# Second block's probabilities split before they are turned, and turned by DMA; score maxima turned by one matmul; places moved

## The chip, the cores and the metric

The kernel runs on one NeuronCore of a Trainium2 chip. The metric is the time of one execution on the device in microseconds (us), lower is better; the time of a kernel is the median of several runs. The engines are TensorE (PE), VectorE (DVE), ScalarE (ACT), GpSimd (POOL) and SyncE (SP), which here only issues DMAs. They run side by side and meet at semaphores.

## What is computed

Eight samples of 512 tokens by 512 channels pass through two transformer blocks. Block 0 has 16 heads of 32 channels and weights rounded to three values; block 1 has one head of 512 channels and full-precision weights. Cut to what matters here:

```python
# block 0: per head, scores by softmax, then values
attn = softmax(einsum('bhqd,bhkd->bhqk', q, k) * hd ** -0.5)
o = einsum('bhqk,bhkd->bhqd', attn, v)
# block 1: one head
Q = h @ q_w + q_b;  K = h @ k_w + k_b;  V = h @ v_w + v_b
attn = softmax(einsum('bnd,bmd->bnm', Q, K) * D ** -0.5)
x = x_in + (einsum('bnm,bmd->bnd', attn, V) @ proj_w + proj_b)
x = x + gelu(film(rmsnorm(x)) @ mlp_w1 + mlp_b1) @ mlp_w2 + mlp_b2
```

## The kernel before, in words

The samples are pipelined: `both(i, j)` on every engine issues block 0 of sample i mixed with block 1 of sample j = i − 1. So there is one pass with block 0 alone, seven mixed ones, and one with block 1 alone. The order of each engine's work is written out by hand: tables such as `S_AT`, `PT_AT`, `PROJ_AT` or `M_AT` give a place (c, n) to each job of block 1, and each engine walks the same list of slots, 24 for c = 0 and 16 for each of c = 1 to 4. In a slot TensorE issues one product of scores by query (L1193; four heads a chunk c, four blocks of 128 queries each), from c = 1 on also one by key (L1243), at set slots the products of probabilities and values (L1278), and what the tables put there. VectorE takes the maximum of each row of scores by query: of two products at once (L1202) for the first 24, of one (L1205) after. ScalarE takes the exponential of each product by key (L1250). The remainder of each probability beyond bf16 is formed on POOL or on VectorE (L1261), as `EXTRA_DVE`, `EXTRA_POOL` and `FIRST_DVE` say: 24 of 64 on VectorE.

The maxima must lie along the free dimension before the scores by key are made. `turn_maxima` turns them with four fp32 transposes of 128×4 (L1212), `max_high` (ACT, L1219) and `max_low` (DVE, L1226) split the turned 4×512 into two bf16 parts, and `stack_maxima` (SP, L1232 and L1234) copies each part by DMA into one row of the stacked queries.

Block 1 works in split bf16: each product is three matmuls a quarter (high by high, high by low, low by high: L1430 to L1432), so an output of 128×512 takes twelve. Its softmax has four row blocks t. `s1` makes the scores, `max1` (L1572 to L1579, DVE) the maximum, `exp_1` (L1589, ACT) the exponential into `wide[t % 2]` in fp32 with its sum. `turn_p1` turns it by four fp32 transposes of 128×128 on TensorE into a PSUM bank (L1600), `p_high` (L1605, ACT) copies that as bf16 and `p_low` (L1611, DVE) subtracts, and `proj1` multiplies both parts with the values. The jobs of block 1 take turns on banks 6 and 7. `exp_1` of t ≥ 2 waits until block t − 2 was turned out of `wide`.

SP issues its DMAs in one order: the weight units of 1 MB (`load_unit`, L1418), for each chunk the parts of queries and keys out to DRAM (L1144, L1146) and back in stacked form (L1155, six), the maxima, and in the MLP of block 0 the transposing DMA of `turn_hidden` (L1380, 128×2048 bf16, 512 KB), which is the only transpose by DMA in the kernel before. POOL forms the values' low parts (`value_low`, L1184) ahead of the remainders.

The wait by which `exp_1` frees its buffer, and the transposes:

```python
            if t >= 2:
                ready(act, plan1, ("pT", t - 2), i)
...
            for k in range(TT):
                mm = pe.transpose(banks[:, b, k * P:(k + 1) * P], wide[:, t % 2, k * P:(k + 1) * P], ident)
```

## Time and profile before

| | us |
|---|---|
| median of 3 runs | 2208.48 |
| lowest, highest | 2206.46, 2213.61 |
| the profiled execution, its own time | 2211.1 |
| its span in the profile | 2209.3 |

The mean granted clock of TensorE in the profiled execution is 0.973 of full speed. The profile gives each engine's busy time, a table of stretches, the chain of work that ended last, groups of instructions by line, and every instruction in order of time. Starts are microseconds from the span's first instruction; "idle before" is what the engine stood idle ahead of an instruction, with the instruction that released it. Instructions overlap: the start of the next one, not the duration, says what one costs its engine.

### The profile page before, as it was taken

How to read it: one execution, taken by the hardware profiler on the slowest of the kernel's cores; microseconds unless marked ns; L12 is line 12 of the kernel's file. 1: busy time of each engine (PE TensorE's matmuls, PEld its weight loads, DVE VectorE, ACT ScalarE, POOL GpSimd, SP SyncE). 2: the span in 40 equal slices, each digit the busy share in tenths (PEclk: the TensorE clock that was granted, in tenths of full speed). 3: DMA queues.
4: the chain of work that ended last, by engine and by line, in shares of the span. 5: the costliest groups of instructions: out<-in, count | busy, mean ns of one | idle time of the engine just before them, and what ended most of it. 6: DMA issues, size and time to landing. Idle time of an engine off the chain costs nothing.

```text
span 2209.3 us, 34388 instructions
## 1 busy us (share of the span) xinstructions
PE 1975.2 (89%) x12991; PEld 981.8 (44%) x12991; DVE 1537.1 (70%) x2667; ACT 1088.2 (49%) x1962; POOL 807.1 (37%) x705
## 2 busy tenths in 40 slices
PE   4787868899988998899988998899988998899989
PEld 3354334544444444544444444544444444544434
DVE  5666567885788767875788767875788767875422
ACT  4475543753456443753456343753456343753230
POOL 2173433741246213741245213741246213741021
PEclk8899889999999999999999999999999999999999
DMA  8442552023321333023321333023321332013212
GB/s 307 146 164 105 191 195 100 26 87 96 129 73 40 105 115 101 26 88 96 132 68 40 107 113 101 26 87 96 131 71 40 109 111 101 26 62 97 91 38 96
DMA packets 152027, 216.97 MB, mean 98 GB/s; under 512 B 74172, under 2 KB 115424, under 8 KB 139704
## 3 DMA queue, kind: packets, MB, share of 16 engines
q1 hardware_dynamic: 144088, 191.66, 26.3%
q10 hardware_dynamic: 7776, 23.10, 2.8%
q8 instruction: 106, 1.74, 0.3%
q14 instruction: 57, 0.47, 0.1%
HBM read 161.97 MB, written 35.72 MB: 89 GB/s over the span
## 4 chain that ended last, share of the span: by engine, by line
PE 55%; DVE 25%; ACT 9%; issue 6%; POOL 3%; DMA 1%; SPq 0%; ACTq 0%; DVEq 0%; POOLq 0%
PE banks L1430 10%; PE banks L1432 10%; PE banks L1431 10%; PE banks L1388 5%; PE banks L1331 4%; DVE memory L1205 4%; PE banks L1278 4%; DVE memory L1202 3%; PE banks L1243 2%; DVE memory L1016 2%; ACT memory L1250 2%; PE banks L1102 2%; PE banks L1193 2%; PE banks L1313 1%; DVE memory L1031 1%
## 5 line engine op out<-in xcount | busy, mean ns | idle before, releaser
L1430 PE MATMUL banks<-memory 128*128 128x512 bf16 x1536 | 586.1, 382 | 25.9 <-DVE memory L1678 5.9
L1431 PE MATMUL banks<-memory 128*128 128x512 bf16 x1536 | 585.5, 381 | 0.0
L1432 PE MATMUL banks<-memory 128*128 128x512 bf16 x1536 | 585.1, 381 | 0.0
L1261 POOL TENSOR_TENSOR memory<-memory 128x512 bf16<-128x512 f32 x332 | 375.4, 1151 | 371.0 <-ACT memory L1250 370.0
L1250 ACT ACTIVATE memory<-banks 128x512 f32<-128x512 f32 x512 | 290.4, 598 | 131.3 <-PE banks L1243 129.1
L1656 POOL TENSOR_TENSOR memory<-memory 128x512 bf16<-128x512 f32 x128 | 153.8, 1204 | 459.1 <-DVE memory L1651 459.1
L1193 PE MATMUL banks<-memory 96*128 96x512 bf16 x512 | 188.6, 395 | 72.8 <-DVE memory L1205 41.4
L1430 PEld LDWEIGHTS banks<-memory 128*128 128x128 bf16 x1536 | 150.7, 98 | 215.3 <-issue 40.0
L1205 DVE TENSOR_REDUCE memory<-banks 128x1 f32<-128x512 f32 x320 | 207.6, 679 | 42.4 <-PE banks L1193 41.9
L1432 PEld LDWEIGHTS banks<-memory 128*128 128x128 bf16 x1536 | 150.8, 98 | 184.0 <-issue 4.4
L1431 PEld LDWEIGHTS banks<-memory 128*128 128x128 bf16 x1536 | 150.9, 98 | 170.5 <-issue 3.5
L1243 PE MATMUL banks<-memory 98*128 98x512 bf16 x512 | 187.6, 391 | 13.3 <-ACT memory L1250 6.7
L1645 ACT ACTIVATE memory<-banks,memory 128x512 f32<-128x512 f32 x128 | 87.5, 684 | 205.1 <-PE banks L1432 135.2
L1678 DVE TENSOR_TENSOR memory<-banks,memory 128x512 f32<-128x512 f32 x128 | 88.2, 689 | 121.3 <-PE banks L1432 120.8
L1278 PEld LDWEIGHTS banks<-memory 128*128 128x128 bf16 x4096 | 145.7, 100 | 47.0 <-issue 24.2
L1261 DVE TENSOR_TENSOR memory<-memory 128x512 bf16<-128x512 f32 x180 | 141.4, 818 | 35.8 <-ACT memory L1250 35.1
L1278 PE MATMUL banks<-memory 128*128 128x66 bf16 x4096 | 152.0, 197 | 14.8 <-issue 12.4
L1651 DVE CAST memory<-memory 128x512 bf16<-128x512 f32 x128 | 67.8, 542 | 93.1 <-ACT memory L1645 92.1
L1331 PE MATMUL banks<-memory 128*128 128x512 fp8e4 x512 | 118.8, 386 | 13.6 <-issue 10.2
L1202 DVE TENSOR_REDUCE memory<-banks 128x2 f32<-128x1024 f32 x96 | 116.8, 1217 | 17.9 <-PE banks L1193 17.1
L1388 PE MATMUL banks<-memory 128*128 128x512 fp8e4 x512 | 118.0, 384 | 8.4 <-DMA memory<-memory 8.4
L1470 POOL TENSOR_TENSOR memory<-memory 128x512 f32<-128x512 f32 x64 | 80.5, 1272 | 119.2 <-DVE memory L1078 112.1
(173 smaller groups left out, 2775.4 us busy)
## 6 DMA issues: line engine op xcount, KB each, us to landing
memory<-weight_parts SPq DMA_DIRECT2D x80, 1024.0 KB, 4.8
memory<-head_parts SPq DMA_DIRECT2D x192, 128.0 KB, 2.6
head_parts<-memory SPq DMA_DIRECT2D x64, 256.0 KB, 2.2
memory<-in_x SPq DMA_DIRECT2D x32, 256.0 KB, 3.4
memory<-ada_rows SPq DMA_DIRECT2D x16, 512.0 KB, 4.5
memory<-in_L_cond_w_fc ACTq DMA_DIRECT2D x2, 4096.0 KB, 14.9
memory<-in_L_cond_mlp_w SPq DMA_DIRECT2D x8, 1024.0 KB, 9.2
weight_parts<-memory SPq DMA_DIRECT2D x8, 1024.0 KB, 5.8
```

The source lines that it names most:

```text
L1193: mm = pe.matmul(banks[:, b], q_stack[0:STACK, c % STACKS, j, t * P:(t + 1) * P], k_stack[0:STACK, c % STACKS, j], start=True, stop=True)
L1202: dve.tensor_reduce(neg_max[:, c % 2, t - 1:t + 1, j], banks[:, b - 1:b + 1], AX.X, ALU.max, negate=True).then_inc(free[b].sem, 1)
L1205: dve.tensor_reduce(neg_max[:, c % 2, t, j:j + 1], banks[:, b], AX.X, ALU.max, negate=True).then_inc(free[b].sem, 1)
L1243: pe.matmul(banks[:, b], k_stack[0:rows, c % STACKS, j, kt * P:(kt + 1) * P], q_stack[0:rows, c % STACKS, j], start=True, stop=True).then_ ...
L1250: act.activation(expo[:, e % RING], banks[:, b], ACT.Exp, scale=HEAD_SCALE).then_inc(free[b].sem, 1)
L1261: eng.tensor_tensor(prob_lo[:, e % RING], expo[:, e % RING], prob_hi[:, e % RING], ALU.subtract).then_inc(ok.sem, 1)
L1278: mm = pe.matmul(banks[:, b, at:at + VALUE], part[:, (h * TT + kt) % RING, t * P:(t + 1) * P], values[:, kt, h], start=(kt == 0 and part i ...
L1331: mm = pe.matmul(banks[:, b], xq[:, k, t * P:(t + 1) * P], w0_fc1[:, k, n * D:(n + 1) * D], start=(k == 0), stop=(k == KC - 1))
L1388: mm = pe.matmul(banks[:, b], hid_turned[t % 2][:, f], w0_fc2[:, f], start=(f == 0), stop=(f == FC - 1))
L1430: pe.matmul(bank, lh, rh, start=(k == 0), stop=False)
L1431: pe.matmul(bank, lh, rl, start=False, stop=False)
L1432: mm = pe.matmul(bank, ll, rh, start=False, stop=(k == KC - 1))
```

## The change

The second block's exponentials are no longer turned in fp32. `p_high` (now on DVE) copies the upper 16 bits of each of `wide`'s words as the high part, `p_low` (now on POOL) subtracts that from the word as the low part, both into a free part of `big`, 128×1024 bf16 for each row block; `turn_p` on SP turns both parts by one transposing DMA of 256 KB into `act_k`, where `proj1` reads them. `exp_1` waits for both parts instead of the turned bank, and the plan has no "pT" jobs. `turn_maxima` turns the 128×16 maxima by one transpose; the parts are split as 16×128. On SP the four transposing DMAs stand behind the third weight unit of a pass, between spill and stack of chunk 2, and ahead of the first maxima. Scores and output products of block 1 can be given in quarters; all quarters of one stand at one slot. Many places move by some slots, and VectorE forms 20 of the 64 remainders.

```diff
-LATE_QK = {(0, 6): ("q", 2), (0, 12): ("k", 2), (1, 3): ("q", 3), (1, 6): ("k", 3)}
+LATE_QK = {(0, 4): ('q', 2), (0, 12): ('k', 2), (1, 2): ('q', 3), (1, 8): ('k', 3)}
...
-M_AT = ((3, 8), (3, 11), (3, 14), (4, 1), (4, 4), (4, 7), (4, 10), (4, 13))
+M_AT = ((3, 11), (3, 13), (3, 15), (4, 2), (4, 3), (4, 5), (4, 9), (4, 15))
...
-TURN_AT = ((2, 7), (2, 9), (2, 11), (2, 13))
-NORM_AT = ((1, 14), (1, 15), (2, 0), (2, 1))
-SQUARE_AT = ((1, 4), (1, 6), (1, 8), (1, 10))
-PT_AT, PT_READ = (((0, 3), (0, 10), (0, 15)), ((0, 2), (0, 11), (0, 14)))
-S_AT = ((0, 4), (0, 7))
-PROJ_AT, PROJ_READ = (((0, 16), (0, 21), (1, 0), (1, 5)), ((0, 15), (0, 22), (0, 23), (1, 5)))
+TURN_AT, FILM_FULL, FILM_HIGH, FILM_LOW = (((2, 5), (2, 7), (2, 9), (2, 12)), ((2, 5), (2, 7), (2, 9), (2, 12)), ((2, 6), (2, 8), (2, 10), (2, 13)), ((2, 7), (2, 9), (2, 11), (2, 14)))
+NORM_AT = ((1, 14), (1, 15), (2, 0), (2, 2))
+SQUARE_AT = ((1, 0), (1, 1), (1, 5), (1, 11))
+PARTS_AT = ((0, 2), (0, 11), (0, 15))
+S_AT, S_MAX, S_EXP = (((0, 4), (0, 4), (0, 4), (0, 4), (0, 8), (0, 8), (0, 8), (0, 8)), ((0, 4), (0, 8)), ((0, 4), (0, 8)))
+PROJ_AT, PROJ_READ = (((0, 16), (0, 16), (0, 16), (0, 16), (0, 20), (0, 20), (0, 20), (0, 20), (1, 0), (1, 0), (1, 0), (1, 0), (1, 5), (1, 5), (1, 5), (1, 5)), ((0, 17), (0, 20), (0, 23), (1, 5)))
...
-MAX_AT = {(0, 17): 0, (1, 8): 1, (2, 11): 2, (3, 10): 3}
+MAX_AT = {(0, 18): 0, (1, 9): 1, (2, 9): 2, (3, 9): 3}
...
-EXTRA_DVE = (17, 22, 25, 30, 34, 38)
-EXTRA_POOL = (48, 52, 56, 60)
+EXTRA_DVE = (12, 14, 17, 23, 34, 38, 39)
+EXTRA_POOL = (46, 48, 49, 50, 54, 56, 57, 60, 62)
...
             b = take(pe, plan0, ("max", c), i)
-            for t in range(TT):
-                mm = pe.transpose(banks[0:G, b, t * P:(t + 1) * P], neg_max[:, c % 2, t], ident)
-            mm.then_inc(full[b].sem, 1)
+            pe.transpose(banks[0:HEADS, b, 0:P], neg_max[:, c % 2].rearrange("p j t -> p (j t)"), ident
+                         ).then_inc(full[b].sem, 1)
...
-            act.activation(max_hi[0:G], banks[0:G, b], ACT.Copy).then_inc(max_parts.sem, 1)
+            act.activation(max_hi[0:HEADS, 0:P], banks[0:HEADS, b, 0:P], ACT.Copy).then_inc(max_parts.sem, 1)
...
             if t >= 2:
-                ready(act, plan1, ("pT", t - 2), i)
+                act.wait_ge(p_hi_ok.sem, p_hi_ok(i, t - 1))
+                act.wait_ge(p_lo_ok.sem, p_lo_ok(i, t - 1))
...
-        def turn_p1(pe, i, t):
-            done(pe, plan1, ("s", t), i)
-            b = take(pe, plan1, ("pT", t), i)
-            for k in range(TT):
-                mm = pe.transpose(banks[:, b, k * P:(k + 1) * P], wide[:, t % 2, k * P:(k + 1) * P], ident)
-            mm.then_inc(full[b].sem, 1)
...
+        def p_high(dve, i, t):
+            done(dve, plan1, ("s", t), i)
+            dve.tensor_copy(p_parts[:, t, 0], wide_hi[:, t % 2]).then_inc(p_hi_ok.sem, 1)
+
+        def p_low(pool, i, t):
+            done(pool, plan1, ("s", t), i)
+            pool.tensor_tensor(p_parts[:, t, 1], wide[:, t % 2], wide_hi[:, t % 2], ALU.subtract
+                               ).then_inc(p_lo_ok.sem, 1)
+
+        def turn_p(sp, i, t):
+
+            sp.wait_ge(p_hi_ok.sem, p_hi_ok(i, t + 1))
+            sp.wait_ge(p_lo_ok.sem, p_lo_ok(i, t + 1))
+            out = act_k[:, :, :, t * P:(t + 1) * P].rearrange("p s k n -> p (s k) n")
+            sp.dma_start_transpose(out, p_parts[:, t].rearrange("p s n -> p (s n)")).then_inc(p_in[t].sem, 16)
...
+                pe.wait_ge(p_in[t].sem, p_in[t](i, 16))
...
                 units(j, 3, 4)
+                if j is not None:
+                    for t in range(2):
+                        turn_p(sp, j, t)
                 if i is not None:
                     spill_parts(sp, i, 2)
+                if j is not None:
+                    turn_p(sp, j, 2)
+                if i is not None:
                     stack_parts(sp, i, 2)
+                if j is not None:
+                    turn_p(sp, j, 3)
+                if i is not None:
                     stack_maxima(sp, i, 0)
...
+                    if j is not None:
+                        p_low(pool, j, 0)
                     for t in range(TT):
                         value_low(pool, i, t)
+                if j is not None:
+                    for t in range(0 if i is None else 1, TT):
+                        p_low(pool, j, t)
...
-                lows1(j, [("s", 1), ("pT", 0)])
+                lows1(j, [("p", 0), ("s", 1)])
...
-                products1(j, [("s", 1), ("pT", 0)])
+                products1(j, [("s", 1)])
```

## Rows read from the trace of the kernel before

**Rows 1.** The page, part 1: busy time, share of the span, instructions

```profile
PE 1975.2 (89%) x12991; PEld 981.8 (44%) x12991; DVE 1537.1 (70%) x2667; ACT 1088.2 (49%) x1962; POOL 807.1 (37%) x705
```

**Rows 2.** Stretches of one sample: from:to, length, busy us (instructions), PEclk, DMA

```profile
1097.00:1127.00 30.00, 24.32 (x117) 10.98 (x115) 25.04 (x36) 6.86 (x15) 2.63 (x3) 1.00 0.38 124
1127.00:1192.00 65.00, 56.27 (x663) 32.41 (x663) 54.85 (x108) 51.46 (x106) 45.95 (x42) 0.95 0.07 22
1192.00:1310.00 118.00, 115.72 (x588) 54.03 (x585) 80.49 (x131) 50.35 (x85) 32.44 (x30) 1.00 0.32 101
```

**Rows 3.** The chain that ended last, 1097 to 1128, by line

```profile
by line: DVE memory L1202 34.0%; issue 8.5%; DVE memory L1626 7.3%; DVE memory L1572 6.5%; DVE memory L1611 6.2%; DVE memory L1126 4.8%; ACT memory L1138 4.7%; DVE memory L1116 4.2%; PE banks L1432 3.5%; PE banks L1193 3.2%; ACT memory L160
```

**Rows 4.** Groups of the whole run by form: busy us, mean ns, idle before

```profile
L1261 POOL TENSOR_TENSOR memory<-memory 128x512 bf16<-128x512 f32 x332 | 375.4, 1151 | 371.0 <-ACT memory L1250 370.0
...
L1651 DVE CAST memory<-memory 128x512 bf16<-128x512 f32 x128 | 67.8, 542 | 93.1 <-ACT memory L1645 92.1
...
L1298 DVE TENSOR_TENSOR memory<-banks,memory 128x128 f32<-128x128 f32 x128 | 32.5, 254 | 0.0
...
L1611 DVE TENSOR_TENSOR memory<-banks,memory 128x512 bf16<-128x512 f32 x32 | 22.0, 687 | 13.4 <-ACT memory L1605 12.4
...
L1226 DVE TENSOR_TENSOR memory<-banks,memory 4x512 bf16<-4x512 f32 x32 | 21.5, 671 | 1.6 <-ACT memory L1219 1.6
...
L1600 PE MATMUL banks<-memory 128*128 128x128 f32 x128 | 19.9, 279 | 11.8 <-ACT memory L1589 11.8
```

**Rows 5.** VectorE in order of time: start, us, line, count, [idle before]

```profile
1097.22 0.69 DVE L1572 TENSOR_REDUCE memory<-banks 128x1 f32<-128x512 f32 x1 [0.82 <-PE banks L1432]
...
1098.26 0.21 DVE L1579 TENSOR_SCALAR memory<-memory 128x1 f32<-128x1 f32 x1
...
1099.81 0.69 DVE L1611 TENSOR_TENSOR memory<-banks,memory 128x512 bf16<-128x512 f32 x1 [1.33 <-ACT memory L1605]
...
1100.42 1.22 DVE L1202 TENSOR_REDUCE memory<-banks 128x2 f32<-128x1024 f32 x1
...
1122.86 1.23 DVE L1202 TENSOR_REDUCE memory<-banks 128x2 f32<-128x1024 f32 x1 [1.66 <-PE banks L1193]
```

**Rows 6.** TensorE in order of time, 1090 to 1130

```profile
1099.43 0.63 PE L1600 MATMUL banks<-memory 128*128 128x128 f32 x4 [1.17 <-ACT memory L1589]
...
1114.07 0.38 PE L1430 MATMUL banks<-memory 128*128 128x512 bf16 x1
...
1126.32 0.38 PE L1243 MATMUL banks<-memory 98*128 98x512 bf16 x1 [0.26 <-DVE memory L1202]
```

**Rows 7.** SP's queue in order of time; DMAs of 1090 to 1150, us to landing

```profile
1101.61 0.43 SPq L1418 DMA_DIRECT2D memory<-weight_parts  x1
...
1116.64 2.92 SPq L1155 DMA_DIRECT2D memory<-head_parts  x6
...
1119.61 0.63 SPq L1232 DMA_DIRECT2D memory<-memory  x1
...
head_parts<-memory SPq DMA_DIRECT2D x6, 256.0 KB, 2.1
...
memory<-weight_parts SPq DMA_DIRECT2D x1, 1024.0 KB, 6.8
```

**Rows 8.** The 512 KB transpose of L1380; its GB/s in slices of 0.2 us

```profile
L1380 SPq DMA_TRANSPOSE memory<-memory x32: 1497/1615/4425, 244.8 to 2029.0; - x32
...
DMA to landing us min/median/max: 3.6/3.7/6.5
...
GB/s 0 0 0 0 0 0 0 0 0 0 0 0 0 173 288 289 292 289 291 292 288 289 213 0 0 0 0 0 0 0 0 0 0 0 0 0 0 0 0 0
```

**Rows 9.** TensorE in the last sample; the stretch 2080 to 2108, columns as rows 2

```profile
2080.98 0.60 PE L1600 MATMUL banks<-memory 128*128 128x128 f32 x4
...
2084.52 0.39 PE L1430 MATMUL banks<-memory 128*128 128x512 bf16 x1 [0.49 <-DVE memory L1611]
...
2080.00:2108.00 28.00, 22.53 (x94) 9.85 (x92) 9.40 (x21) 7.33 (x18) 0.00 (x0) 0.88 0.00 1
```

More of the change, by code:

```diff
@@ L327, in two_blocks @@
         h_amax, h_inv, h_quant, h_deq = fp32(TT), fp32(TT), fp32(TT), fp32(TT)
-        neg_max = fp32(2, TT, G)
+        neg_max = fp32(2, G, TT)
         sum_inv = fp32(TT, H)
@@ L407, in two_blocks @@
         inv1 = signal("inv1", 4)
-        pT_hi = signal("pT_hi", 4)
+        p_hi_ok, p_lo_ok = signal("p_hi_ok", TT), signal("p_lo_ok", TT)
+        p_in = [signal(f"p_in{t}", 16) for t in range(TT)]
         g1_hi = signal("g1_hi", 16)
@@ L1225, in max_low @@
             dve.wait_ge(max_parts.sem, max_parts(i, c + 1))
-            dve.tensor_tensor(max_lo[0:G], banks[0:G, b], max_hi[0:G],
+            dve.tensor_tensor(max_lo[0:HEADS, 0:P], banks[0:HEADS, b, 0:P], max_hi[0:HEADS, 0:P],
                               ALU.subtract).then_inc(free[b].sem, 1)
@@ L1560, in qv_low, with s1 @@
                                   ALU.subtract).then_inc(free[b].sem, 1)
-        def s1(pe, i, t):
+        def s1(pe, i, t, ks=range(KC)):
             if t == 0:
                 all_done(pe, plan1, [("q", c) for c in range(KC)], i, ("s", t))
-            b = take(pe, plan1, ("s", t), i)
+            b = take(pe, plan1, ("s", t), i) if ks[0] == 0 else plan1["s", t][0]
             cols = slice(t * P, (t + 1) * P)
             three_terms(pe, banks[:, b], lambda k: (act_q[:, 0, k, cols], act_q[:, 1, k, cols]),
-                        lambda k: (act_h[:, 0, k], act_h[:, 1, k]), full[b])
+                        lambda k: (act_h[:, 0, k], act_h[:, 1, k]), full[b], ks)
         def max1(dve, i, t):
@@ L1594, in invert1 @@
             dve.reciprocal(suminv1[:, t:t + 1], sum1[:, t:t + 1]).then_inc(inv1.sem, 1)
-        def turn_p1(pe, i, t):
-            done(pe, plan1, ("s", t), i)
-            b = take(pe, plan1, ("pT", t), i)
-            for k in range(TT):
-                mm = pe.transpose(banks[:, b, k * P:(k + 1) * P], wide[:, t % 2, k * P:(k + 1) * P], ident)
-            mm.then_inc(full[b].sem, 1)
-        def p_high(act, i, t):
-            b = ready(act, plan1, ("pT", t), i)
-            act.activation(act_k[:, 0, :, t * P:(t + 1) * P],
-                           banks[:, b].rearrange("p (k n) -> p k n", k=TT), ACT.Copy).then_inc(pT_hi.sem, 1)
@@ L1618, in proj1 @@
+        def proj1(pe, i, t, ks=range(KC)):
+            if ks[0] == 0:
+                all_done(pe, plan1, [("v", TT - 1)], i, ("proj", t))
+                pe.wait_ge(p_in[t].sem, p_in[t](i, 16))
+            b = take(pe, plan1, ("proj", t), i) if ks[0] == 0 else plan1["proj", t][0]
             cols = slice(t * P, (t + 1) * P)
             three_terms(pe, banks[:, b], lambda k: (act_k[:, 0, k, cols], act_k[:, 1, k, cols]),
-                        lambda k: (act_v[:, 0, k], act_v[:, 1, k]), full[b])
+                        lambda k: (act_v[:, 0, k], act_v[:, 1, k]), full[b], ks)
@@ L1695, in two_blocks @@
         Q, V = ([(w, c) for c in range(KC)] for w in "qv")
-        s_p = lambda s_at, p_at: [(at, ("s", t + 2)) for t, at in enumerate(s_at)] + [
-            (at, ("pT", t + 1)) for t, at in enumerate(p_at)]
-        PE_AT = place(*s_p(S_AT, PT_AT), *((at, ("proj", t)) for t, at in enumerate(PROJ_AT)),
+        quarters = lambda name, first, places: [(at, (name, first + k // KC, (k % KC,))) for k, at in enumerate(places)]
+        PE_AT = place(*quarters("s", 2, S_AT), *quarters("proj", 0, PROJ_AT),
                       *((at, ("turn", k)) for k, at in enumerate(TURN_AT)), *((at, (*M[k // KC], (k % KC,))) for k, at in enumerate(M_AT)))
-        DVE_AT = place(*s_p(S_AT, PT_READ), *((at, ("proj", t)) for t, at in enumerate(PROJ_READ)),
-                       *((later(at, 2), ("low", k)) for k, at in enumerate(TURN_AT)))
-        ACT_AT = place(*s_p(S_AT, PT_READ), *((at, ("square", t)) for t, at in enumerate(SQUARE_AT)),
+        DVE_AT = place(*((at, ("s", t + 2)) for t, at in enumerate(S_MAX)),
+                       *((at, ("p", t + 1)) for t, at in enumerate(PARTS_AT)), *((at, ("proj", t)) for t, at in enumerate(PROJ_READ)),
+                       *((at, ("low", k)) for k, at in enumerate(FILM_LOW)))
+        ACT_AT = place(*((at, ("s", t + 2)) for t, at in enumerate(S_EXP)), *((at, ("square", t)) for t, at in enumerate(SQUARE_AT)),
                        *((at, ("norm", t)) for t, at in enumerate(NORM_AT)),
-                       *((at, ("full", k)) for k, at in enumerate(TURN_AT)),
-                       *((later(at, 1), ("film", k)) for k, at in enumerate(TURN_AT)))
+                       *((at, ("full", k)) for k, at in enumerate(FILM_FULL)),
+                       *((at, ("film", k)) for k, at in enumerate(FILM_HIGH)))
         @block.sync
@@ L1932, in both @@
                         value_high(act, i, t)
-                highs1(j, [("s", 1), ("pT", 0)])
+                highs1(j, [("s", 1)])
                 for c, n in slots():
```

47 lines of the change are left out of this document (19 added, 28 removed).

## The prediction

> **What bounds the kernel now.** I read the page's busy shares first, then a table of stretches of one sample, then the chain, the groups and the order of time in the stretch that changes. TensorE (PE) is busy for 89% of the span, VectorE (DVE) for 70% [rows 1], but the stages differ. Steady samples repeat every 248 us with the same waits, and there are seven in which one sample's first block runs beside the previous sample's second. In the one shown, 1192 to 1310 is PE alone (115.7 of 118 us); 1127 to 1192 has PE 56.3, DVE 54.9 and ACT 51.5 of 65, three engines that hand banks round, with POOL at 46.0; and 1097 to 1127, where the second block's softmax lies, has DVE 25.0 and PE 24.3 of 30 [rows 2]. There the chain is VectorE's: 34% of it is the maxima of score pairs (L1202), and PE's lines are small shares [rows 3]. So in the first 24 slots a microsecond taken off DVE's list is a microsecond of the sample, if PE's list shrinks as much; and then everything moves left, since what follows is PE-bound.
>
> **The probabilities, first 24 slots.** Removed per sample: 16 fp32 transposes on PE (19.9 us over 128, so 0.62 a group of four in the busy column; in order of time the next matmul starts 0.43 after a group), four ACT copies, and four DVE subtractions of 0.687, which follow each other at 0.60 [rows 4]. Added: four DVE copies, four POOL subtractions, four transposing DMAs on SP. Step by step on DVE:
>
> - Start. Today DVE finishes the second score block's maximum at 1098.26 + 0.21 = 1098.47, then idles 1.33 for ACT's copy of the first turned block, subtracts, and begins the first pair at 1100.42. In the change the first split needs no turned block: it goes ahead of that maximum, where 0.82 us are idle already. The pairs can start at 1098.47: 1.95 us [rows 5].
> - Three further subtractions at 0.60 become copies. The nearest row is the fp32 to bf16 cast, 0.542 [rows 4], 0.47 at the same overlap: 3 × 0.13 = 0.4 us. The input has a step of two; bounds 0.3 a copy (a gain of 0.9 us) and 0.75 (a loss of 0.4).
> - The low part of the maxima shrinks from 512 columns (0.671, paced 0.60) to 128; nearest row the 128-column add from PSUM, 0.254, paced 0.18 [rows 4]: 0.4 us.
> - DVE idles once more, 1.66 us before 1122.86, because PE put a whole output product between two scores of a pair [rows 5]. The new place (0,20) is ahead of a pair, not inside it. I take half, 0.8; bounds 0 and 1.7.
>
> Sum 3.5 us. PE must shed as much: four groups at 0.43, its wait of 1.17 at the second group [rows 6], and three of the four transposes of maxima (like those, so 0.33) make 3.2, and it idles 5.7 of 30 us here. So 3.5 us for this stretch, bounds 2.5 and 4.9. ACT, 6.9 busy of 30 [rows 2], isn't in it.
>
> **What the moved work waits for.** SP issues the weight unit at 1101.61 and the first transpose only then, behind 1 MB that lands 6.8 us later, at 1108.4 [rows 7]. How long 256 KB take isn't in this trace; 512 KB take 1.5 to 4.4 us of SP (median 1.6), land in 3.7 and move for some 1.9 us at 288 GB/s [rows 8]. So the first lands between 1108.4 + 0.9 = 1109.3 and 1108.4 + 3.7 = 1112.1; I take 1110.3, since half the bytes cost half of the moving part and the fixed part runs under the load. The first output product starts at 1114.07 now [rows 6], and in the change 2.2 us earlier, at 1111.9, or at 1110.6 if PE gets its banks sooner. No wait. The other three are due at slot (0,20) and in the next chunk, each further off. POOL's parts are in time: it is busy 2.6 of 30 us here [rows 2]; the first subtraction (1.15, the row for its like [rows 4]) goes ahead of the four of the values, and the later ones find it idle.
>
> Behind SP's waits are queued the spill and stack of the third chunk's parts and the first maxima. Today the six stack DMAs start at 1116.64 and the first of two maxima DMAs at 1119.61, while the first matmul that needs them runs at 1126.32 [rows 6, 7]. After: the stack ends 2.2 us earlier, at 1117.3, the last transpose takes 1.6, the maxima 1.2, landing 2.1 (the 256 KB spill, nearest row [rows 7]): 1122.3, against 1126.3 − 3.5 = 1122.8. No wait, by half a microsecond. The maxima's DMA has 16 runs in place of 4 with the same 4 KB; I take the same price.
>
> **Slots of 1127 to 1192.** PE sheds 3 × 0.33 = 1.0 us of transposes of maxima, DVE 3 × 0.42 of their low parts, ACT a little of their high parts; and DVE gives four of its 24 probability remainders net to POOL, whom they cost 4 × 1.15 = 4.6 [rows 4]. POOL has 19 us free there, but DVE gets two more early (remainders 12 and 14) and fewer late. Three engines wait in turn, so I take what PE loses, 1.0; bounds 0 and 2. The moved places of squares, norms, film and fc1 quarters issue what they issued before, under PE's idle 8.7 us of these chunks [rows 2]: nothing, and if that cover is gone 0.65 us (one quarter, three matmuls) a sample.
>
> **Ends.** The last sample's second block runs alone. There no product runs from 2080.98 to 2084.52, because PE waits for what stands on both sides of its transposes, and the same happens again 10.4 us on: twice 3.54. And PE's granted clock is 0.88 of full in those 28 us, that is, it falls to its lower level (1.2 of 2.4 GHz) after each gap, which costs 0.12 × 28 = 3.4 us [rows 9]. Together 10.5. In the change split and transposes lie under products of 2.6 us each; I take 10, bounds 5 and 10.5. The first sample has only its maxima: 1 us, bounds 0.5 and 1.5.
>
> **Sum.** 7 × (3.5 + 1.0) + 10 + 1 = 42.5 us. Against the profiled execution's own 2211.1: 2168.6. That execution lies 2.6 above the median of 2208.5, so 2166. By the lower bounds (7 × 3.0 + 5 + 0.5) 26.5 us, 2182; by the upper (7 × 6.9 + 10.5 + 1) 59.8, 2149.
>
> **Rivals.** (1) *The first transpose is late.* It lands at 1112.1, PE is ready at 1110.6 and waits 1.5; the maxima behind the transposes cost another 0.8. For it: one SP queue and 1 MB ahead; against: 288 GB/s for a transpose alone. 7 × 2.2 + 8 + 1 = 24.4 us: 2184. Chance 0.17.
> (2) *The exchange in the later slots costs.* Remainders 12 and 14 delay maxima that free PE's banks, or POOL, 46 of 65 busy [rows 2], is late for the value products; 2 us a sample are given back: 7 × 2.5 + 11 = 28.5: 2180. Chance 0.12. For it: PE already idles 8.7 us there; against: DVE's whole list gets shorter.
> (3) *Slower: the transposes hold SP.* Stack and maxima stand behind them in one queue. For an issue of X, 1102.4 + 3X + 2.9 + X + 1.2 + 2.1 = 1108.6 + 4X is when the maxima have landed; it decides from X = 4.4, where that passes 1126.3. The longest issue in the row is 4.4, the median 1.6 for twice the bytes [rows 8], which speaks against. At 6.5, the longest landing, they are 8.3 us late in seven samples and nothing is won at the end: 2208.5 + 58 = 2266. Chance 0.05.
> The Trainium skill speaks for this side: "VectorE: DVE Perf Modes", section "Rules for kernel authors", would turn a 128×128 block on TensorE where PSUM will do and gives (section "The three transpose paths") 1.31 us by DMA against 0.39. An estimate from that page is 10.5 us for eight blocks one after another, the fourth set at 1144, some 15 us lost a sample and a time above 2300. The trace disagrees: 16 blocks land in 3.7 us [rows 8].
> (4) *A new wait takes all of it back* (transposes and maxima both some 3 us later than taken): 2203 to 2215, chance 0.06.
>
> **How the numbers follow.** Forecast 0.60, rivals 0.17, 0.12, 0.05 and 0.06. The time is the forecast's, 2166. The range 2149 to 2190 takes in the forecast's bounds and rivals 1 and 2; it leaves out rivals 3 and 4 and what falls outside the bounds. About 0.3% (6.6 us) is what a measurement of this kernel can tell from no change. Rival 4 lies mostly within it. Faster 0.90, within 0.3% 0.04, slower 0.06.
>
> **What would show it.** Right: the first L1202 of a steady sample follows the second block's maximum within 0.3 us; no wait for a DMA before the first output product; the 24 slots some 3.5 us shorter; transposes of half the size landing in 2 to 3 us; in the last sample no holes of 3.5 us and a granted clock near 1. Wrong: a PE wait whose releaser is a DMA, at the output products (rival 1) or at the first by-key product behind long DMA_TRANSPOSE issues (rival 3), or more idle before L1193 and the value products in the later slots (rival 2).

## The result, and the profile after

| | before | after |
|---|---|---|
| median of the runs | 2208.59 us (2206.46 to 2213.61, 4 runs) | 2156.81 us (2151.24 to 2160.13, 4 runs) |
| ratio, 95% interval | | 0.976 [0.9733, 0.9787] |
| profiled execution, span | 2211.1, 2209.3 | 2151.24, 2149.4 |

The kernel is 51.8 us faster by the medians, 59.9 by the two profiled executions (the profiled one of after is the fastest of its four). The forecast was 42.5. Two runs that took far longer than their like, 3346 us of the changed kernel with the old shares and 5149.5 us of the kernel before, are left out of the ratios below. First the page of the changed kernel, parts 1 and 4:

```profile
PE 1938.8 (90%) x12767; PEld 953.8 (44%) x12767; DVE 1528.6 (71%) x2639; ACT 1058.1 (49%) x1930; POOL 885.2 (41%) x765
...
PE 57%; DVE 22%; ACT 8%; issue 5%; POOL 4%; DMA 3%; SPq 1%; ACTq 0%; DVEq 0%; POOLq 0%
```

Against [rows 1] PE is 36 us less busy. DVE ran 28 instructions fewer and is busy only 8.5 us less, POOL is busy 78 us more.

**Where the time went.** A steady sample is measured best from ScalarE's load of the Exp table, which opens the second block's softmax, to its next table load, which closes the attention stretch. Between them I took the start of the first pair of maxima (L1202, in the changed kernel L1205), of the first single maximum (L1205, in the changed kernel L1208: the end of the 24 slots) and of the first by-key product (L1243, in the changed kernel L1247) of each chunk. Means of the seven samples, and the last one:

| us | before | after | forecast of the change |
|---|---|---|---|
| table load to first pair | 7.7 | 5.8 | -1.95 |
| table load to first single maximum | 34.5 | 30.3 | -3.5 |
| from there to the next table load | 63.1 | 59.8 | -1.0 |
| last sample, between its table loads | 44.4 | 34.2 | -10 |
| start of the execution to the first such load | 348.6 | 349.4 | -1 |

The second line holds the first. Seven times 4.1 + 3.3, and 10.2, make about 62. The stretches in which PE runs alone gave back 0.3 a sample and the first one 0.8, and what stands behind the last sample won 0.4: about 60, which is the profiled difference of 59.9. Against the forecast the third line has 16 us more (7 × 2.3), the second 4, and the first sample and the stretches of PE alone take 4 back.

The stretches of the changed kernel, with the columns of [rows 2] (from:to, length, busy us of PE, PEld, DVE, ACT and POOL, granted clock, DMA). The first, second and fourth are the 24 slots of three samples, from the first of the pairs to the first by-key products; the third is the sequel of the second:

```profile
836.10:860.30 24.20, 20.92 (x95) 8.62 (x93) 23.16 (x35) 3.93 (x9) 6.13 (x6) 1.00 0.80 196
1075.70:1101.30 25.60, 22.09 (x94) 8.95 (x92) 22.53 (x34) 3.93 (x9) 6.13 (x6) 0.93 0.70 185
1101.30:1161.30 60.00, 52.46 (x647) 29.54 (x646) 55.11 (x102) 48.77 (x104) 51.28 (x46) 1.00 0.08 24
1317.00:1343.10 26.10, 23.21 (x93) 9.03 (x91) 22.52 (x34) 3.93 (x9) 6.11 (x6) 0.87 0.82 182
2031.00:2045.00 14.00, 14.00 (x67) 6.35 (x65) 6.78 (x19) 4.22 (x12) 4.87 (x4) 1.00 0.34 76
```

The later slots took 60.0 us for the 64.2 of the same work before (1126.3 to 1190.5), with DVE as busy as then and POOL 5 us busier. And the 24 slots come in two lengths: about 24 us at a granted clock of 1.00, about 26 below it. From table load to first single maximum they took 29.2 to 29.9 in the four samples at 1.00 and 31.3 to 31.8 in the three at 0.87 to 0.93, where the kernel before took 34.4 or 34.5 in all seven. The last line is the last sample, where the holes of [rows 9] stood: PE is busy for 14.00 of 14.00 us, at full clock. There the transposes are wholly hidden.

VectorE in order of time, the sample of 1070.7:

```profile
1076.38 0.21 DVE L1583 TENSOR_SCALAR memory<-memory 128x1 f32<-128x1 f32 x1
1076.51 1.22 DVE L1205 TENSOR_REDUCE memory<-banks 128x2 f32<-128x1024 f32 x1
1077.64 1.07 DVE L1603 COPY memory<-memory 128x512 bf16<-128x512 bf16 x1
...
1088.82 0.41 DVE L1603 COPY memory<-memory 128x512 bf16<-128x512 bf16 x1
...
1094.39 1.23 DVE L1205 TENSOR_REDUCE memory<-banks 128x2 f32<-128x1024 f32 x1 [1.89 <-PE banks L1196]
...
1096.48 0.27 DVE L1228 TENSOR_TENSOR memory<-banks,memory 16x128 bf16<-16x128 f32 x1
```

And the sample of 831.1, one at full clock:

```profile
852.76 1.22 DVE L1205 TENSOR_REDUCE memory<-banks 128x2 f32<-128x1024 f32 x1 [0.21 <-PE banks L1196]
```

The first pair follows the second block's maximum at once: the idle 1.33 before L1611 in [rows 5] is gone. The idle 1.66 of [rows 5] is 0.21 in this sample and 1.89 in the one above. In all seven: 0.21 three times and 0.90 in the samples at full clock, 1.89, 2.65 and 2.80 in the others. TensorE in the same two samples shows why:

```profile
1089.48 0.59 PE L1434 MATMUL banks<-memory 128*128 128x512 bf16 x1
1089.87 0.63 PE L1435 MATMUL banks<-memory 128*128 128x512 bf16 x1
1090.29 0.63 PE L1436 MATMUL banks<-memory 128*128 128x512 bf16 x1
...
1101.27 0.38 PE L1247 MATMUL banks<-memory 98*128 98x512 bf16 x1
```

```profile
849.53 0.38 PE L1434 MATMUL banks<-memory 128*128 128x512 bf16 x1
849.75 0.38 PE L1435 MATMUL banks<-memory 128*128 128x512 bf16 x1
```

The output products' first matmuls come 0.43 us apart in the one and 0.22 in the other: the lower of TensorE's two levels (1.2 GHz) against the upper (2.4). Ahead of them PE had waited three times for maxima in both samples (1.07, 1.19 and 1.14 us; 1.07, 0.84 and 1.14). Neither has a DMA wait before the first output product; two of the seven have one, of 0.58 us (the sample of 588.7) and 0.52 (that of 1556.9).

SP's queue in the sample of 1070.7, then the transposes of the whole run (ns min/median/max of one issue), their landings, and who waited for them:

```profile
1079.39 0.43 SPq L1422 DMA_DIRECT2D memory<-weight_parts  x1
1079.93 7.31 SPq L1615 DMA_TRANSPOSE memory<-memory  x2
...
1096.24 0.59 SPq L1234 DMA_DIRECT2D memory<-memory  x1
...
L1615 SPq DMA_TRANSPOSE memory<-memory x32: 1231/1462/5005, 358.1 to 2040.6; - x32
...
  PEld banks L1434: 2.4, 3
  PE banks L1434: 1.1, 2
...
DMA to landing us min/median/max: 2.7/3.7/9.6
```

These medians mix different cases. In the last sample, with nothing else moving, each of the four transposes costs SP 1.2 us and lands in 2.7, a microsecond sooner than the 512 KB of [rows 8]. In a steady sample the first, behind the 1 MB of weights, lands 8.3 to 9.6 us after its issue, the second after 6.0 to 7.9, the other two after 2.7 to 3.8; the first two hold SP together for 7.2 to 8.4. In the whole run PE's products waited 1.1 us for them, and its weight loads, which overlap products, 2.4.

The groups that changed, as in [rows 4]:

```profile
L1265 POOL TENSOR_TENSOR memory<-memory 128x512 bf16<-128x512 f32 x360 | 413.1, 1171 | 217.8 <-ACT memory L1254 214.4
...
L1265 DVE TENSOR_TENSOR memory<-memory 128x512 bf16<-128x512 f32 x152 | 143.2, 964 | 30.7 <-ACT memory L1254 29.1
...
L1607 POOL TENSOR_TENSOR memory<-memory 128x512 bf16<-128x512 f32 x32 | 36.3, 1134 | 119.5 <-ACT memory L1594 119.5
L1603 DVE COPY memory<-memory 128x512 bf16<-128x512 bf16 x32 | 20.7, 646 | 2.2 <-ACT memory L1594 2.2
L1228 DVE TENSOR_TENSOR memory<-banks,memory 16x128 bf16<-16x128 f32 x32 | 8.7, 272 | 3.4 <-ACT memory L1221 3.4
```

DVE's remainders (L1265) are 152 for 180 and as busy in total as before (141.4 us then): one takes 964 ns for 818. The DVE copy of the split takes 0.41 us by itself. The first two of each steady sample take 0.8 and 1.05 us: they start while POOL is in a low part of the values (L1187). In the last sample three copies start 0.04 us ahead of POOL's L1607 and take 0.43.

### The profile page after: what moved, and what is told of

The parts are those of the page before. It is cut to its first block, busy times and chain, and to the rows that moved or that the text cites. A ratio compares the mean times of both kernels' runs of the same rounds, so it can differ in the third digit from the quotient of the medians.

```text
span 2149.4 us, 33988 instructions
## 1 busy us (share of the span) xinstructions
PE 1938.8 (90%) x12767; PEld 953.8 (44%) x12767; DVE 1528.6 (71%) x2639; ACT 1058.1 (49%) x1930; POOL 885.2 (41%) x765
## 4 chain that ended last, share of the span: by engine, by line
PE 57%; DVE 22%; ACT 8%; issue 5%; POOL 4%; DMA 3%; SPq 1%; ACTq 0%; DVEq 0%; POOLq 0%
PE banks L1434 10%; PE banks L1436 10%; PE banks L1435 10%; PE banks L1335 5%; PE banks L1392 5%; DVE memory L1208 4%; PE banks L1282 3%; POOL memory L1265 2%; PE banks L1247 2%; DVE memory L1019 2%; ACT memory L1254 2%; DMA memory<-memory 2%; PE banks L1196 2%; DVE memory L1034 2%; PE banks L1105 2%
## 5 line engine op out<-in xcount | busy, mean ns | idle before, releaser
L1265 POOL TENSOR_TENSOR memory<-memory 128x512 bf16<-128x512 f32 x360 | 413.1, 1171 | 217.8 <-ACT memory L1254 214.4
L1660 POOL TENSOR_TENSOR memory<-memory 128x512 bf16<-128x512 f32 x128 | 153.0, 1198 | 479.5 <-DVE memory L1655 479.5
L1196 PE MATMUL banks<-memory 96*128 96x512 bf16 x512 | 182.9, 391 | 64.7 <-DVE memory L1208 36.9
L1208 DVE TENSOR_REDUCE memory<-banks 128x1 f32<-128x512 f32 x320 | 207.1, 679 | 21.6 <-PE banks L1196 21.3
L1247 PE MATMUL banks<-memory 98*128 98x512 bf16 x512 | 185.9, 386 | 14.3 <-ACT memory L1254 7.0
L1265 DVE TENSOR_TENSOR memory<-memory 128x512 bf16<-128x512 f32 x152 | 143.2, 964 | 30.7 <-ACT memory L1254 29.1
L1282 PE MATMUL banks<-memory 128*128 128x66 bf16 x4096 | 147.5, 194 | 18.8 <-POOL memory L1265 13.9
L1655 DVE CAST memory<-memory 128x512 bf16<-128x512 f32 x128 | 61.1, 486 | 110.8 <-ACT memory L1649 109.8
L1335 PE MATMUL banks<-memory 128*128 128x512 fp8e4 x512 | 119.0, 387 | 13.1 <-issue 9.7
L1205 DVE TENSOR_REDUCE memory<-banks 128x2 f32<-128x1024 f32 x96 | 115.3, 1214 | 15.9 <-PE banks L1196 15.1
```

Source lines behind the costliest of these rows:

```text
L1196: mm = pe.matmul(banks[:, b], q_stack[0:STACK, c % STACKS, j, t * P:(t + 1) * P], k_stack[0:STACK, c % STACKS, j], start=True, stop=True)
L1208: dve.tensor_reduce(neg_max[:, c % 2, j, t:t + 1], banks[:, b], AX.X, ALU.max, negate=True).then_inc(free[b].sem, 1)
L1247: pe.matmul(banks[:, b], k_stack[0:rows, c % STACKS, j, kt * P:(kt + 1) * P], q_stack[0:rows, c % STACKS, j], start=True, stop=True).then_ ...
L1265: eng.tensor_tensor(prob_lo[:, e % RING], expo[:, e % RING], prob_hi[:, e % RING], ALU.subtract).then_inc(ok.sem, 1)
L1282: mm = pe.matmul(banks[:, b, at:at + VALUE], part[:, (h * TT + kt) % RING, t * P:(t + 1) * P], values[:, kt, h], start=(kt == 0 and part i ...
L1335: mm = pe.matmul(banks[:, b], xq[:, k, t * P:(t + 1) * P], w0_fc1[:, k, n * D:(n + 1) * D], start=(k == 0), stop=(k == KC - 1))
```

## The experiments

What had to be told apart: whether the split and the transposes made the gain, as the forecast had it, or the moved places and the exchange of remainders, which it had costed at nothing. Medians are set against the kernel before on the same chip: 2207.14 for the first four kernels below, up to the changed one with the old shares; 2211.16 for the exchange alone, the places of chunk 1 and later, the four transposes in the changed kernel and the doubled DMAs; 2208.59 for the other four. The changed kernel wasn't run beside them, so comparisons with it go by the ratios. The stretches come from one profiled execution of each kernel.

### The three parts by themselves

**One matmul for the maxima, alone** (kernel before):

```diff
-            for t in range(TT):
-                mm = pe.transpose(banks[0:G, b, t * P:(t + 1) * P], neg_max[:, c % 2, t], ident)
-            mm.then_inc(full[b].sem, 1)
+            pe.transpose(banks[0:HEADS, b, 0:P], neg_max[:, c % 2].rearrange("p j t -> p (j t)"), ident
+                         ).then_inc(full[b].sem, 1)
...
```

> The kernel before with one change: the maxima are turned by one transpose of 128x16 and split as 16x128. Theory (the work taken off the engines' lists is what shortens the attention part): TensorE sheds 0.33 us in each of 32 chunks, 10 us in all, and the low parts on VectorE 0.4 us each in chunk 0 of seven samples; 8 to 13 us faster than before. Rival (the late slots' gain came from places and from the exchange with POOL): 0 to 4 us faster, since the transposes of the maxima lay in waits of TensorE.

2219.81 us (6 runs), ratio 1.0056 [1.0039, 1.0073]: 12.7 us slower, which neither theory had. Work was taken off three engines. The 24 slots are as before (34.5); the later ones take 64.2 for 63.1. DVE, POOL and PE in chunk 2, the third, of one sample:

```profile
1163.12 1.28 DVE L1205 TENSOR_REDUCE memory<-banks 128x1 f32<-128x512 f32 x2
1164.31 1.20 DVE L1503 TENSOR_TENSOR memory<-memory 128x512 bf16<-128x512 f32 x1
1165.43 1.52 DVE L1262 TENSOR_TENSOR memory<-memory 128x512 bf16<-128x512 f32 x1
1166.88 0.68 DVE L1205 TENSOR_REDUCE memory<-banks 128x1 f32<-128x512 f32 x1
...
1169.73 0.68 DVE L1262 TENSOR_TENSOR memory<-memory 128x512 bf16<-128x512 f32 x1
...
1165.18 2.67 POOL L1262 TENSOR_TENSOR memory<-memory 128x512 bf16<-128x512 f32 x2 [0.21 <-ACT memory L1251]
...
1167.62 0.61 PE L1193 MATMUL banks<-memory 96*128 96x512 bf16 x1 [2.56 <-DVE memory L1205]
```

Two DVE operations that take 0.67 us elsewhere took 1.20 and 1.52 between two maxima, the second of them started 0.25 us after a remainder on POOL; PE idled 2.56 us for the maximum behind them, and its next product ran at the lower clock level (0.61 for 0.39). This stretch shows how taking work away can cost time; that it makes up the whole 12.7 us is not shown.

**The split and the transposes, alone** (the changed kernel with the old places, the old shares and the maxima by four transposes; one line of the edit):

```diff
-PARTS_AT = ((0, 2), (0, 11), (0, 15))
+PARTS_AT = ((0, 2), (0, 11), (0, 14))
```

> The changed kernel with all places, shares and the turning of the maxima as before: only the probabilities' split and transposing DMAs are new. Theory: the first pair of maxima starts 2 us earlier in a sample, the 24 slots shrink by 2.5 to 3.5 us, the last sample by 10: 28 to 36 us faster than before. Rival (the places are needed to take the time out): 10 us from the last sample and 1 us a sample, 14 to 20 faster.

2188.03 us, ratio 0.9919 [0.9889, 0.9948]: 19.1 us faster. First pair at 5.8, the 24 slots 33.1, the later ones 62.2, last sample 34.9. The size is the rival's. So the last sample gives 9.5 us and a steady one 2.4, of which the start is 2.0. The start gain and the end are the transposes'; little else of the forecast's steady sample is.

**All places and the exchange, alone** (the kernel before with every constant of the diff that it has, its own functions; some of its lines):

```diff
-MAX_AT = {(0, 17): 0, (1, 8): 1, (2, 11): 2, (3, 10): 3}
+MAX_AT = {(0, 18): 0, (1, 9): 1, (2, 9): 2, (3, 9): 3}
...
-PROJ_AT, PROJ_READ = (((0, 16), (0, 21), (1, 0), (1, 5)), ((0, 15), (0, 22), (0, 23), (1, 5)))
+PROJ_AT, PROJ_READ = (((0, 16), (0, 20), (1, 0), (1, 5)), ((0, 17), (0, 20), (0, 23), (1, 5)))
...
-EXTRA_POOL = (48, 52, 56, 60)
+EXTRA_POOL = (46, 48, 49, 50, 54, 56, 57, 60, 62)
```

> The kernel before at the new places and with the new share of remainders on POOL, its turning of probabilities and maxima untouched. Theory: the places are no gain by themselves, within 5 us of before either way. Rival (places and exchange made the 2.3 us a sample in the late slots that the forecast lacks): 12 to 18 us faster than before.

2175.36 us, ratio 0.9851 [0.9826, 0.9876]: 31.8 us faster, more than either theory had and the largest part by far. First pair 7.8 and last sample 44.3 as before; the 24 slots 32.6 and the later ones 59.0 for 63.1. With the 19.1 of the parts alone it makes 50.9 of the 51.8. The kernel that has both and lacks only the maxima by one matmul stands below ("Its maxima by four transposes again"): it is 53.5 us faster than the kernel before on its chip.

### Which of the places, and what the exchange is worth

**Back to the old shares, in the changed kernel:**

```diff
-EXTRA_DVE = (12, 14, 17, 23, 34, 38, 39)
-EXTRA_POOL = (46, 48, 49, 50, 54, 56, 57, 60, 62)
+EXTRA_DVE = (17, 22, 25, 30, 34, 38)
+EXTRA_POOL = (48, 52, 56, 60)
```

> The changed kernel with the shares of remainders as before: 24 of 64 on VectorE in place of 20. Theory: the exchange is worth at most 0.5 us a sample, so 0 to 4 us slower than the changed kernel, 2157 to 2161 us. Rival (VectorE is what sets the last chunks, and 3.3 us less on it are worth most of that): 10 to 20 us slower than the changed kernel, 2167 to 2177.

2165.01 us (3 runs), ratio 0.9805 [0.9776, 0.9833], for 0.976 [0.9733, 0.9787] of the changed kernel: 8 us slower by the medians and 10 by the ratios, just clear of the two intervals taken together, and between theory and rival. The later slots take 61.2 for 59.8. The exchange is worth some 9 us there.

**The exchange alone, in the kernel before** (the same two lines, the other way):

> The kernel before with only the two sets of remainders of the change: VectorE 20 of 64 in place of 24. Theory (the places, not the exchange, made the 32 us of the run that had both): within 6 us of before, because VectorE's operations lengthen beside POOL's. Rival (the exchange is most of it): 10 to 20 us faster. That the changed kernel loses 9 us without the exchange speaks for about that here too.

2223.32 us, ratio 1.0049 [1.0033, 1.0066]: 12.2 us slower, which neither theory had. The 24 slots take 35.0 for 34.5 and the later ones 63.7 for 63.1. The same exchange has two signs.

**Only the places of chunk 1 and later, with the cuts of the wide work, in the kernel before** (two lines of the edit):

```diff
-DVE_CUTS = (2, 3, 4, 6, 8, 9, 10, 11, 12)
-BOUNDS = (14, 14, 15, 16, 17, 18, 19, 20, 21, 22, 23, 24, 25, 26, 27, 27)
+DVE_CUTS = (2, 3, 3, 6, 7, 9, 10, 11, 12)
+BOUNDS = (14, 14, 15, 17, 17, 18, 19, 20, 20, 21, 23, 23, 24, 26, 27, 27)
```

> The kernel before with the change's places from slot (1,0) on (third and fourth query and key parts, maxima 1 to 3, squares, norms, film, the eight quarters of the first MLP products and the cuts after them), all of the first 24 slots and the shares as before. Theory: these places take the waits out of chunks 1 to 3, where the run with all places gained 4 us a sample: 12 to 24 us faster than before. Rival (they are neutral and the exchange did it): within 5 us of before.

2212.84 us (10 runs), ratio 1.0005 [0.9992, 1.0018]: no change, as the rival had it. But inside a sample much moves, as the table below shows.

**Only the places of the first 24 slots, in the kernel before** (one line of the edit):

```diff
-S_AT = ((0, 4), (0, 7))
+S_AT = ((0, 4), (0, 8))
```

and with it the quarter at (0, 20), the reads, the first maxima at (0, 18) and 'q' 2 at (0, 4) and (0, 5).

> The kernel before with the new places of the first 24 slots alone: second score block at (0,8), projection quarter at (0,20) with its reads, the reads at (0,15), the 'q' 2 works at (0,4) and (0,5), the three maxima works at (0,18). Later places and the shares of the remainders stay. The new places with the new shares were worth 32 us, the shares alone cost 12, the places from chunk 1 on with their cuts alone brought nothing. Theory (the gains of the parts add up): the first 24 slots carry 32 + 12 = 44 us, so 2160 to 2172. Rival (the pieces only work together: each sample keeps the 1.5 to 2 us that the first 24 slots get shorter and nothing behind them): 10 to 15 us faster, 2196 to 2201. Third (PE puts the saved time into longer waits of chunk 1): no change.

2201.79 us (10 runs), ratio 0.9971 [0.9961, 0.9981]: 6.8 us faster. The 24 slots fell from 34.5 to 32.4, 2.1 a sample; the later ones rose from 63.1 to 63.9 (the profiled execution is the slowest of the ten, 4.9 us above their median). So the theory that the gains of the pieces add up, which wanted 37 to 49 us, is wrong.

**All places, old shares, in the kernel before:**

> The kernel before with all new places and cuts, but with the old shares of the remainders (EXTRA sets). If the exchange of remainders costs by itself what it costs in the kernel before (12 us), this is 44 us faster than before, 2160 to 2168. If the exchange is worth what it is in the changed kernel (9 us), it is 23 us faster, 2184 to 2190. If the exchange is what makes the new places pay at all, it is within 8 us of before.

2194.60 us, ratio 0.9941 [0.9929, 0.9954]: 14.0 us faster, which is between the second theory and the third. With the new shares on top it is 2175.36. So in the kernel before, as ratios:

| | old shares | new shares | the exchange |
|---|---|---|---|
| old places | 1 | 1.0049 | +0.5% |
| new places | 0.9941 | 0.9851 | -0.9% |
| changed kernel (new places) | 0.9805 | 0.976 | -0.45% |

What places and exchange do shows chunk by chunk, each from its first by-key product to the next chunk's. Shortest and longest of seven samples in us:

| | chunk 1 | chunk 2 | chunk 3 |
|---|---|---|---|
| kernel before | 18.5 to 20.1 | 17.3 to 18.3 | 14.7 to 16.1 |
| late places alone | 17.5 to 17.6 | 20.1 to 21.4 | 13.1 to 15.0 |
| early places alone | 18.5 to 19.9 | 17.3 to 21.4 | 13.7 to 15.8 |
| all places, old shares | 17.5 to 17.6 | 20.3 to 21.4 | 13.1 to 15.1 |
| all places, new shares | 17.5 to 17.6 | 17.0 | 13.3 to 13.5 |

The late places shorten chunks 1 and 3 and lengthen chunk 2 by about as much; that is why they alone are worth nothing. The exchange, at these places, takes chunk 2 back to 17.0 in every sample. The early places alone make chunk 2 longer in five samples of seven, where part of their gain goes. Chunk 2 of one sample with all places and the old shares, and DVE and POOL in it:

```profile
1142.00:1162.50 20.50, 15.93 (x181) 9.59 (x182) 18.18 (x34) 17.46 (x35) 16.33 (x16) 0.94 0.13 40
...
1143.15 0.18 DVE L1297 RECIPROCAL memory<-banks 128x4 f32<-128x4 f32 x1 [1.04 <-ACT memory L1291]
...
1145.76 0.92 DVE L1261 TENSOR_TENSOR memory<-memory 128x512 bf16<-128x512 f32 x1 [0.46 <-ACT memory L1250]
...
1151.07 1.52 DVE L1261 TENSOR_TENSOR memory<-memory 128x512 bf16<-128x512 f32 x1
...
1154.57 1.04 POOL L1261 TENSOR_TENSOR memory<-memory 128x512 bf16<-128x512 f32 x1 [1.08 <-ACT memory L1250]
...
1161.20 1.78 POOL L1261 TENSOR_TENSOR memory<-memory 128x512 bf16<-128x512 f32 x1 [1.68 <-ACT memory L1250]
```

The same stretch with the new shares:

```profile
1131.30:1148.30 17.00, 13.88 (x180) 8.88 (x181) 16.52 (x33) 15.99 (x32) 15.97 (x14) 1.00 0.16 48
...
1134.27 5.90 POOL L1261 TENSOR_TENSOR memory<-memory 128x512 bf16<-128x512 f32 x5 [0.39 <-ACT memory L1250]
...
1139.78 0.93 DVE L1261 TENSOR_TENSOR memory<-memory 128x512 bf16<-128x512 f32 x1
1140.43 8.54 POOL L1261 TENSOR_TENSOR memory<-memory 128x512 bf16<-128x512 f32 x7 [0.26 <-ACT memory L1250]
```

Between these two by-key products, in all seven samples of each kernel: DVE forms 2 remainders (1.6 us) for 3 or 4 (3.4 to 4.7 us) and waits for ScalarE 0.2 us for 1.7 to 2.0; POOL waits for ScalarE 1.2 us for 4.1 to 5.6, so it works in long rows; and the granted clock is 1.00 for 0.89 to 0.94. That is 3.3 to 4.4 us in one chunk, of which the stretch behind chunk 3 gives 0.5 back (11.7 for 11.2). These go together; which of them is the cause, and which of the moved numbers brings it about, was not tried. Of the clock alone an estimate is 0.06 × 20.5 = 1.2 us in the sample shown.

### The changed kernel's own parts

**Its maxima by four transposes again** (the first diff backwards, in the changed kernel):

> The changed kernel with its maxima turned by four transposes and split as 4x512. Theory (after a run in which one transpose alone made the kernel before slower): TensorE has waits there anyway, so within 6 us of the changed kernel, 2151 to 2163. Rival (the forecast's 1.3 us a sample for the maxima is real at the new places): 8 to 13 us slower, 2165 to 2170.

2157.62 us, ratio 0.975 [0.9728, 0.9772]: the same time, as the theory had it. What cost 12.7 us in the old schedule is worth nothing that can be told here.

**Every transposing DMA issued twice**, SP waiting for the first to land and PE for the second:

```diff
-            sp.dma_start_transpose(out, p_parts[:, t].rearrange("p s n -> p (s n)")).then_inc(p_in[t].sem, 16)
+            for n in range(2):
+                if n:
+                    sp.wait_ge(p_in[t].sem, p_in[t](i, 16))
+                sp.dma_start_transpose(out, p_parts[:, t].rearrange("p s n -> p (s n)")).then_inc(p_in[t].sem, 16)
```

> The changed kernel with each of the four transposing DMAs issued, waited for on SP and issued again, so that SP is held for about 4 us more each and the products wait for the second. Theory: the first output product, which now starts without a wait, waits 2 to 4 us and the first maxima go out 8 us or more later, some 6 us a sample lost: 35 to 60 us slower than the changed kernel. Rival (the transposes have more room than the forecast gave them): less than 15 us slower.

2243.18 us, ratio 1.0131 [1.0102, 1.016]: by the ratios 82 us slower than the changed kernel, more than the theory's 35 to 60, and slower than before. SP's queue, PE and the 24 slots of one sample:

```profile
1120.31 14.73 SPq L1618 DMA_TRANSPOSE memory<-memory  x4
...
1136.28 4.18 SPq L1618 DMA_TRANSPOSE memory<-memory  x2
...
1147.83 0.59 SPq L1234 DMA_DIRECT2D memory<-memory  x1
...
1132.47 0.61 PE L1434 MATMUL banks<-memory 128*128 128x512 bf16 x1 [2.69 <-DMA memory<-memory]
...
1150.21 0.61 PE L1247 MATMUL banks<-memory 98*128 98x512 bf16 x1 [5.11 <-DMA memory<-memory]
...
1115.40:1150.40 35.00, 24.29 (x93) 9.35 (x94) 23.91 (x36) 3.94 (x9) 6.15 (x6) 0.81 0.67 168
```

PE waits for DMAs at both places that the prediction named, 2.69 us at the output products and 5.11 at the first by-key product, behind SP. Over the run its products wait 23.0 and 39.1 us for DMAs at these two lines, for 1.1 and 3.5 in the changed kernel: 57.5 of the 82. The clock falls to 0.81 in this stretch. This is rival 3 as it would have looked. All but one of the second issues land in 2.7 us.

**The first maxima's DMAs ahead of the fourth transpose:**

```diff
+                if i is not None:
+                    stack_maxima(sp, i, 0)
                 if j is not None:
                     turn_p(sp, j, 3)
                 if i is not None:
-                    stack_maxima(sp, i, 0)
                     spill_parts(sp, i, 3)
```

> The changed kernel with SP's order altered at one point: the two DMAs of the first chunk's maxima go ahead of the fourth transposing DMA (1.2 to 1.3 us of SP). Theory (the maxima's landing ends PE's wait at the first by-key products, 1.1 us at 1119.4 in the profile of the changed kernel): 0.5 to 1 us a sample, 3 to 8 us faster than the changed kernel. Rival (the SP waits on the low part of the maxima, so the transpose is held instead and the last output product waits for it): 3 to 10 us slower. No change if neither is on the path.

2157.16 us, ratio 0.9769 [0.9756, 0.9783]: no change. I had misread the wait that I named: 1119.4 is the second chunk's first by-key product, and its maxima go by another pair of DMAs. The first chunk's stood at 1101.27 without a DMA wait; over the seven samples it waited twice, 0.12 and 0.22 us.

**The low parts of the probabilities on VectorE:**

```diff
             dve.tensor_copy(p_parts[:, t, 0], wide_hi[:, t % 2]).then_inc(p_hi_ok.sem, 1)
+            p_low(dve, i, t)
...
-                    if j is not None:
-                        p_low(pool, j, 0)
...
-                if j is not None:
-                    for t in range(0 if i is None else 1, TT):
-                        p_low(pool, j, t)
```

> The changed kernel with the four low parts of the second block's probabilities subtracted on VectorE right behind each copy, instead of on POOL. The prediction costed POOL's four at nothing and took the 24 slots as VectorE's list. Theory (VectorE bounds there): four subtractions of 0.6 us, 2.4 us a sample, less 0.4 to 0.6 each that the copies beside POOL are lengthened: 0 to 2 us a sample in seven samples, so up to 14 us slower than the changed kernel. Rival (the subtraction stands ahead of the first pair of maxima and holds PE's banks: 2.4 us and more a sample): 17 to 25 us slower. If POOL's overlap costs as much as it saves: no change.

2162.74 us (4 runs), ratio 0.9788 [0.9772, 0.9804], for 0.976 [0.9733, 0.9787]: 6 us slower than the changed kernel, which the two intervals taken together don't tell from nothing. The 24 slots take 31.6 for 30.3, and 30.9 or 31.0 for 29.2 to 29.9 in the samples at full clock: some 1.5 us for four subtractions of 0.71. VectorE's list does bound there, but the copies are shorter than beside POOL (578 ns for 646).

No run was faster than the changed kernel by more than the intervals tell.

## Why the prediction was right, and where it was wrong

The sign, the range and the size held (2156.8 against 2166, range 2149 to 2190). The account did not: a part of the change that was costed at nothing made more than half of the gain, and terms that were costed turned out smaller. That the sum came so near is in part luck.

**Right.** *Start*, 1.95 us: 2.0 in six samples, 1.2 in the seventh. *Ends*, 10 us: 10.2, and 9.5 with the transposes alone, no hole and a full clock. *No wait for the first transpose*: 1.1 us over the run, in two samples. *Nothing in the way of the first maxima*: 0.3 us over the run, and going earlier brings nothing. *Landing of half the size in 2 to 3 us*: 2.7 with nothing else moving. The first of a sample lands 8.3 to 9.6 us after its issue, for 7.9 taken and bounds of 6.9 to 9.7. *POOL's parts are in time*: the first output product waits for none. Mis-sized was what the first two transposes hold SP: 7.2 to 8.4 us together, where the forecast went by a median of 1.6 each. It fell into a margin that was there; doubling the transposes shows that the margin is a few microseconds of SP.

**Sizes that were off in the 24 slots.** The forecast had 3.5, measured were 4.1, a mean of two kinds of sample. The step "I take half, 0.8" had the wrong shape: the idle 1.66 goes mostly (0.21 to 0.90) at full clock and not at all (1.89 to 2.80) below it. The copies saved less than 0.13 each: 646 ns on average against 687 for what they replace. But with the transposes alone the 24 slots gave only 1.4 us, below the lower bound of 2.5; the rest of the 4.1 needs the new places.

**A slip in the sum of the lower bounds.** It has 3.0 us a steady sample, where its terms are 2.5 and 0. By them it is 7 × 2.5 + 5.5 = 23 us, 2185.5 and not 2182. The four DVE terms at their own bounds give 2.0 us, not 2.5. The stated range holds either.

**The step that failed: "The moved places … issue what they issued before … nothing".** The moved places and the exchange alone are worth 31.8 us in the kernel before, against nothing. That an instruction is issued as often says nothing of a stage in which three engines hand banks round. The forecast's rival 2, that the exchange costs, had the right place and a mechanism that exists: it costs 12 us at the old places. At the new ones it gains: chunk 2 falls to 17.0 us, with POOL and DVE hardly waiting for ScalarE and full clock. Neither follows from busy sums. Why the places alone give 14 us is partly shown: 2 us a sample are won in the first 24 slots, and what the late places win in chunks 1 and 3 chunk 2 takes back.

**The step "I take what PE loses, 1.0".** PE's three transposes less a chunk were worth nothing (ratio 0.975 with the four, 0.976 without), and in the old schedule their removal cost 12.7 us. The 3.3 us that the later slots gained come from the places and the exchange, which give 4.1 without the new maxima or the DMAs. The forecast's 7 us for this had the right sign and the wrong source. The same holds for the *first sample*, 1 us forecast: nothing was won (-0.8), and this first stretch differs by some microseconds between kernels that do the same in it (345.2 to 355.0), so it can't be read that finely.

**Turning on TensorE or by DMA.** The Trainium skill, "VectorE: DVE Perf Modes", section "Rules for kernel authors", would keep 128×128 turns on TensorE where PSUM will do. The trace disagrees in the last sample, where eight blocks a DMA are hidden under products; with each DMA issued twice the advice would have been right (ratio 1.0131). What decides here is the room in SP's queue before the first reader.

**Open.** Why the 24 slots keep full clock in four samples of seven and not in the other three, with nearly the same waits ahead of them; which of the remainders' numbers carry the exchange; and whether the lower clock makes chunk 2 long or follows from its waits.

## What to carry to other kernels

Where several engines hand the same buffers round and all are some 80 to 87% busy, an edit of the order is not free because it issues the same work: try it alone, at both settings of whatever else moves, since here one exchange changed the time by -19, -9 and +12 us. Taking work away can cost time there. What can be read off a trace beforehand are waits with a named releaser: the two that this change removed (at the start of a sample, on average, and in the last one) came out within 0.3 us.
